# Reading out a linear-attention memory as one block of tiled matmuls instead of riders between gate/up matmuls

## The reference

```python
log_f_cum = jnp.cumsum(jax.nn.log_sigmoid(fg), axis=-1)
log_D = jnp.where(ltr, log_f_cum[..., :, None] - log_f_cum[..., None, :] + ig[..., None, :], -jnp.inf)
max_log_D = jnp.max(log_D, axis=-1, keepdims=True)
C = jnp.einsum('bhsd,bhtd->bhst', qh, kh) / jnp.sqrt(jnp.float32(dh)) * jnp.exp(log_D - max_log_D)
normalizer = jnp.maximum(jnp.abs(jnp.sum(C, axis=-1, keepdims=True)), jnp.exp(-max_log_D))
h = jnp.einsum('bhst,bhtd->bhsd', C / (normalizer + EPS_BACKEND), vh)
...
x = x + _L0_xattn_ref(_layernorm(x, axis=-1), ctx_1024, ctx_1024, ...)
x = x + _L0_ffn_ref(_layernorm(x, axis=-1), w_gate, w_up, w_down)   # fp4_linear: 512 -> 1408 (twice), silu(gate) * up, 1408 -> 512
```

## Time and profile before

| | |
|---|---|
| median of 3 runs | 1887.38 us (1887.36 to 1887.93) |
| the profiled execution | 1892.68 us, its span 1891.0 us |
| TensorE busy | 1783.6 us (94%), mean granted clock 0.971 |
| VectorE busy | 1566.1 us (83%) |
| ScalarE busy | 1415.8 us (75%) |
| GpSimd busy | 1191.7 us (63%) |
| one plain turn | 26.41 us |
| one gate turn | 28.98 us |

### The profile page before, as it was taken

The page is one execution under the profiler, slowest core; times in us unless marked ns, Lnnn a source line. Parts: engine busy times, 40 slices in busy tenths (PEclk is TensorE's granted clock), DMA queues, the critical chain, the costliest instruction groups (busy, mean ns, idle before and its releaser), DMA issues. The chain is left out here.

```text
span 1891.0 us, 36967 instructions
## 1 busy us (share of the span) xinstructions
PE 1783.6 (94%) x11513; PEld 1046.0 (55%) x11513; DVE 1566.1 (83%) x3213; ACT 1415.8 (75%) x2943; POOL 1191.7 (63%) x1189
## 2 busy tenths in 40 slices
PE   4557999999999999999999999999999999999996
PEld 3434556556555565555556555655565555555553
DVE  8987888888887888879888888888888888889993
ACT  7765777787877777777777877777787877776753
POOL 7765666566666656666666666656666665656652
PEclk8668999999999999999999999999999999999998
DMA  6334454344444534444444454444443454445332
GB/s 214 101 75 94 120 115 111 108 120 124 108 114 114 127 99 116 120 111 116 113 121 109 121 115 116 109 110 119 123 110 108 122 126 101 115 104 110 88 66 62
DMA packets 342116, 211.47 MB, mean 112 GB/s; under 512 B 275200, under 2 KB 281856, under 8 KB 341920
## 3 DMA queue, kind: packets, MB, share of 16 engines
q1 hardware_dynamic: 341920, 209.10, 44.1%
HBM read 125.93 MB, written 17.30 MB: 76 GB/s over the span
## 5 line engine op out<-in xcount | busy, mean ns | idle before, releaser
L485 PE MATMUL bank<-wgTh,xqT 128*128 128x512 f16 (+1 forms) x1536 | 556.9, 363 | 15.0 <-DMA xqT<-xqs 15.0
L485 PE MATMUL bank<-wuTh,xqT 128*128 128x512 f16 (+1 forms) x1536 | 556.6, 362 | 0.0
L1077 POOL TENSOR_TENSOR stage<-stage,hs 128x512 f32<-128x512 f32 (+1 forms) x192 | 190.4, 992 | 433.9 <-DVE stage L1286 433.9
L613 PE MATMUL bank<-wdTh,work 128*128 128x512 f16 x704 | 269.0, 382 | 12.3 <-DMA work<-stage 12.2
L485 PE MATMUL bank<-wgTl,xqT 128*128 128x512 f16 (+1 forms) x768 | 278.4, 362 | 0.0
L485 PE MATMUL bank<-wuTl,xqT 128*128 128x512 f16 (+1 forms) x768 | 278.1, 362 | 0.0
L614 PE MATMUL bank<-wdTl,work 128*128 128x512 f16 x704 | 267.7, 380 | 0.0
L615 PE MATMUL bank<-wdTh,work 128*128 128x512 f16 x704 | 267.4, 380 | 0.0
L485 PEld LDWEIGHTS bank<-wgTh,xqT 128*128 128x128 f16 x1536 | 157.1, 102 | 160.0 <-DMA xqT<-xqs 22.7
L1130 POOL TENSOR_TENSOR stage<-stage,hinv 128x512 f32<-128x512 f32 (+1 forms) x192 | 238.9, 1246 | 8.2 <-DVE hinv L1371 8.1
L485 PEld LDWEIGHTS bank<-wuTh,xqT 128*128 128x128 f16 x1536 | 163.8, 107 | 131.8 <-issue 1.1
(11 more groups left out here) (209 smaller groups left out, 3954.4 us busy)
## 6 DMA issues: line engine op xcount, KB each, us to landing
mb<-max_dram SPq DMA_DIRECT2D x64, 512.0 KB, 4.0
x<-in_x_dram SPq DMA_DIRECT2D x64, 256.0 KB, 2.9
cf<-in_ctx_dram SPq DMA_DIRECT2D x64, 256.0 KB, 3.7
cn<-in_ctx_dram SPq DMA_DIRECT2D x64, 256.0 KB, 3.8
wb<-warp_dram SPq DMA_DIRECT2D x128, 128.0 KB, 3.4
out_dram<-ob SPq DMA_DIRECT2D x64, 256.0 KB, 3.7
xb<-in_x_dram SPq DMA_DIRECT2D x60, 256.0 KB, 2.6
work<-stage SPq DMA_TRANSPOSE x192, 3.1
```

The lines of the kernel that those rows point to most:

```text
L485: i = e.matmul(o[:, 0:width], x, w[:, c, n0:n0 + width], start=first and k < 2, stop=last and k >= 4)
L613: e.matmul(DOWN[:, :], hi, wdT[0][:, c0 + c, :], start=(c0 + c == 0), stop=False)
L1077: e.tensor_tensor(blocks(hx[:, n0:n0 + w]), blocks(hx[:, n0:n0 + w]), per_block(hs2[:, n0 // BLOCK:(n0 + w) // BLOCK]), ALU.mult).then_inc ...
```

## The change

The riders go. u becomes a block of its own behind the third gate/up piece, followed at once by `pe_st_mm`, which was behind down part 0. Inside the block every product is cut to a half of the output rows (64 columns of the array). The product with the old memory reads `St` itself: 64 rows of one head by 64 columns, so that four such matmuls use the four quarters of the array (16 matmuls). The product of `D` and `vc` uses all 128 rows and one half of the columns each (16 matmuls). `U` is laid out anew: even heads in bank R2, odd heads in bank R0, and `act_uc` writes with a stride. `Sbd`, its two copies per tile and its semaphores go. The memory is updated in one pass of four instructions, one for each head pair (`St*wb + ST`), at the place of the old `dve_St`; `sp_wb_in` waits for it.

```diff
-        U = [b[:, 0:HC * DA].rearrange("p (c r d) -> p c r d", r=2, d=DA) for b in (R2, R0)]
+        U = [b[:, 0:HC * DA].rearrange("p (c d) -> p c d", d=DA) for b in (R2, R0)]
+        HALF = [slice(0, P // 2), slice(P // 2, P)]
...
             if t.has(1):
-                e.wait_ge(S_["Sd"], t.done(1))
+                e.wait_ge(S_["St"], t.done(1))
                 e.wait_ge(S_["xw"], t.done(1))
...
-                    if n == 2 and c >= 2 and t.has(2) and rider.live(NT):
-                        pe_u_part(e, rider, 6 * (c - 2) + k)
...
-        def pe_u_part(e, t, k):
...
-            c, j = divmod(k, 3)
-            o = U[c // 2][:, c % 2]
-            if j == 0:
-                return e.matmul(o.rearrange("p r d -> p (r d)"), xw[:, c, :], Sbd[:, c, :, :].rearrange("p r d -> p (r d)"),
-                                start=(c % 2 == 0), stop=False)
-            i = e.matmul(o[:, j - 1, :], D[:, j - 1, c, :], vc[t.parity][:, 2 * c + j - 1, :], start=False, stop=(c % 2 == 1 and j == 2))
...
+        def pe_u(e, t):
...
+            if t.has(8):
+                e.wait_ge(S_["St"], t.done(8))
+            e.wait_ge(S_["xw"], t.done())
+            for c in range(HC):
+                for half in HALF:
+                    for par in range(2):
+                        r = slice(par * DH, (par + 1) * DH)
+                        e.matmul(U[par][half, c, :], xw[r, c, half], St[t.slot][r, c, :], start=(c == 0), stop=False)
+            e.wait_ge(S_["vc"], t.done())
+            e.wait_ge(s_C[0], t.done())
+            e.wait_ge(s_C[1], t.done())
+            for c in range(HC):
+                for par in range(2):
+                    for half in HALF:
+                        i = e.matmul(U[par][half, c, :], D[:, par, c, half], vc[t.parity][:, 2 * c + par, :], start=False, stop=(c == HC - 1))
+            i.then_inc(S_["u"], 1)
...
             if t8.live(NT):
                 pe_gu(e, t8, 2)
+            if t6.live(NT):
+                pe_u(e, t6)
+                pe_st_mm(e, t6)
             if t9.live(NT):
                 pe_down(e, t9, 0)
-            if t6.live(NT):
-                pe_st_mm(e, t6)
...
-        def act_Sbd(e, t, par):
...
-            e.copy(uc[:, HC * k:HC * (k + 1), :], U[k].rearrange("p c r d -> p (c r) d")).then_inc(s_uc[k], 1)
+            e.copy(uc[:, :, :].rearrange("p (c r) d -> p r c d", r=2)[:, k], U[k]).then_inc(s_uc[k], 1)
...
-        def dve_Sd(e, t):
+        def dve_St(e, t):
...
             e.wait_ge(S_["wb_in"], t.of(32, 31))
+            e.wait_ge(S_["u"], t.done())
+            e.wait_ge(S_["st_mm"], t.done())
...
-            e.tensor_tensor(St[t.slot][:, :, :], St[t.slot][:, :, :], per_head(wb[:, :, P - 1], DA), ALU.mult).then_inc(S_["Sd"], 1)
...
-            e.tensor_tensor(St[t.slot][:, :, :], ST, St[t.slot][:, :, :], ALU.add).then_inc(S_["St"], 1)
+            for c in range(HC):
+                i = e.scalar_tensor_tensor(St[t.slot][:, c, :], St[t.slot][:, c, :], wb[:, c, P - 1:P], ST[:, c, :], ALU.mult, ALU.add)
+            i.then_inc(S_["St"], 1)
```

More of the change, by code:

```diff
@@ L259, in mlstm_fp4_ffn @@
             "row3", "row4", "mc", "row_T", "cols",
-            "D", "xw", "vc", "vk", "qk", "u", "st_mm", "Sd", "St", "sq", "un",
+            "D", "xw", "vc", "vk", "qk", "u", "st_mm", "St", "sq", "un",
             "nrm", "vr", "ve", "sch", "hn", "x1",
@@ L275, in mlstm_fp4_ffn @@
         s_gu, s_silu, s_h = ([S_[f"{k}{n}"] for n in range(NP)] for k in ("gu", "silu", "h"))
-        s_mask, s_C, s_uc, s_Sbd = ([sem(f"s_{k}{n}") for n in range(2)] for k in ("mask", "C", "uc", "Sbd"))
+        s_mask, s_C, s_uc = ([sem(f"s_{k}{n}") for n in range(2)] for k in ("mask", "C", "uc"))
         s_hx, s_hz, s_h_t, s_h_q, s_h_qs, s_h_hi = ([sem(f"s_{k}{n}") for n in range(NP)] for k in ("hx", "hz", "h_t", "h_q", "h_qs", "h_hi"))
@@ L474, in pe_gu @@
                 e.wait_ge(s_h[n + 1], t.done(1))
-            rider = t.back(-2)
             for c in range(EC):
@@ L557, in pe_pick_mm @@
                 i.then_inc(S_["pick_mm"], 1)
-        def pe_u_part(e, t, k):
+        def pe_u(e, t):
             later = t.back(-5)
[L562 to L574, removed]
-            c, j = divmod(k, 3)
-            o = U[c // 2][:, c % 2]
-            if j == 0:
-                return e.matmul(o.rearrange("p r d -> p (r d)"), xw[:, c, :], Sbd[:, c, :, :].rearrange("p r d -> p (r d)"),
-                                start=(c % 2 == 0), stop=False)
-            i = e.matmul(o[:, j - 1, :], D[:, j - 1, c, :], vc[t.parity][:, 2 * c + j - 1, :], start=False, stop=(c % 2 == 1 and j == 2))
-            return i.then_inc(S_["u"], 1) if k == 11 else i
@@ L583, in pe_u @@
-        def pe_u(e, t):
-            for k in range(12):
-                pe_u_part(e, t, k)
+            if later.live(NT + 1) and later.slot % 4 == 0 and later.has(4):
+                e.wait_ge(S_["cols"], later.quads(4))
+            if later.live(NT):
+                e.wait_ge(S_["xT"], later.done())
+                if later.at_start(7):
+                    e.wait_ge(S_["gr"], later.quads_of(4, 3))
+            if t.at_start(0):
+                e.wait_ge(S_["zero"], 1)
+            if t.has(8):
+                e.wait_ge(S_["St"], t.done(8))
@@ L1048, in act_start @@
             e.preload_act_table_set(EXP_LN); act_f_exp(e, T[7]); act_uc(e, T[2], 1); act_x_hi(e, T[1]); act_f_log(e, T[7]); act_uc(e, T[2], 0); act_hz(e, T[0], 1)
-            act_sq(e, T[2]); act_D(e, T[3]); act_warp(e, T[7]); act_hz(e, T[0], 2); act_hz(e, T[0], 0); act_ln1_sq(e, T[8]); act_Sbd(e, T[3], 1)
-            act_silu(e, T[1], 0); act_h_hi(e, T[0], 0); act_nm2(e, T[2]); act_Sbd(e, T[3], 0); act_sq2(e, T[2]); act_ln1_var(e, T[8]); act_var2(e, T[2])
+            act_sq(e, T[2]); act_D(e, T[3]); act_warp(e, T[7]); act_hz(e, T[0], 2); act_hz(e, T[0], 0); act_ln1_sq(e, T[8])
+            act_silu(e, T[1], 0); act_h_hi(e, T[0], 0); act_nm2(e, T[2]); act_sq2(e, T[2]); act_ln1_var(e, T[8]); act_var2(e, T[2])
             act_x1c(e, T[2]); act_silu(e, T[1], 1); act_xh(e, T[8]); act_h_hi(e, T[0], 1); act_silu(e, T[1], 2); e.preload_act_table_set(EXP_LN)
@@ L1176, in pool_zero @@
                 e.memset(St[i][:, :, :], 0.0)
-            e.memset(Sbd[:, :, :, :], 0.0)
             for i in range(2):
@@ L1615, in dve_turn @@
                 dve_x_t(e, t7)
-            if t6.live(NT):
-                dve_Sd(e, t6)
             if t1.live(NT):
@@ L1699, in dve_start @@
             dve_x_q(e, T[2]); dve_ht(e, T[1]); dve_nr_neg(e, T[3]); dve_h_lo(e, T[0], 2); dve_nr(e, T[3]); dve_nq(e, T[3]); dve_vr(e, T[3]); dve_hm(e, T[1])
-            dve_n2(e, T[3]); dve_x_lo(e, T[2]); dve_ve(e, T[3]); dve_Sd(e, T[3]); dve_hinv(e, T[1]); dve_St(e, T[3]); dve_hn(e, T[3])
+            dve_n2(e, T[3]); dve_x_lo(e, T[2]); dve_ve(e, T[3]); dve_hinv(e, T[1]); dve_St(e, T[3]); dve_hn(e, T[3])
         @block.vector
```

31 lines of the change are left out of this document (10 added, 21 removed).

## The result

The changed kernel has a median of 1878.33 us (1876.42 to 1880.88, 6 runs) against 1889.52 us for the kernel before on the same chips; the ratio is 0.9939, 95% interval 0.9923 to 0.9956. It is faster by 0.6%, where 1.8% was forecast, and 1878.33 us lies 1.3 us above the range. The profiled execution went from 1892.7 to 1876.4 us: 16.3 us, where the sum said 33.3.

The account below looks back on a forecast made before the run. TensorE's list was taken to bound each turn; plain turns 29.1, late transposes 4.1, tail turns 3.6, gate turns -3.5 and start-up 0 sum to 33.3 us gained: 1859.4 us profiled, 1854 median (-1.8%), range 1842 to 1877.

Parts of the forecast that it names:

- each term of the block: New TensorE block: memory product 0.47, D times vc 0.94, pe_st_mm 0.47, changes of form 0.36; together 2.24 us against 2.95.
- four quarters at once: Memory product in the new block: 32 records, four at a time, 8 steps, taken as 0.47 us; bounds up to 1.87.
- The third `act_silu`: ScalarE in plain turns: silu 2 moves up 1.2 us and no more, because it waits 1.19 us for TensorE.
- The rival of pairs: Memory product's quarters run two at a time: 0.94 us, gain 0.24 us a turn, 1876 us; chance 0.14 including an in-between case.
- the serial quarters: Rival: quarters in the memory product don't overlap, 1.87 us, block 3.64 us; slower, 1925 us; chance 0.11.
- The rule of some 25 ns between starts: Skill's limit on matmul starts: the memory product's 32 records would need 0.80 us, gain 0.38 us a turn.
- The sentence on SyncE's wait for the update: SyncE's wait for St before wb_in stands behind the x transpose, issue 1.2 us, so St is done by then.
- The bound of -2 to +2 us: Start-up put at 0 within these bounds: VectorE and ScalarE lose short instructions, but the first update stands later.
- Late transposes: Plain turns: the x transpose's margin grows from 1.04 to 1.5 us, covering the 1.4 us excess; 4.1 us gained.
- VectorE's 1.28 us: Plain turns: VectorE loses the 1.28 us decay pass, 1.2 as a step, so its work moves up 1.2 us.
- Gate turns: In 14 turns the scores wait for St, which ends 0.76 us after its start; each 0.25 us longer, -3.5 us.
- The base: Profiled execution of 1892.7 us, 5.3 above the median; the same gain was taken from both, giving 1859.4 and 1854 us.

Follow-up runs that it names:

- e1: Changed kernel with the load of tile 3's decay factors moved behind tile 1's x transpose in SyncE's start-up list; 1865.19 us, ratio 0.9863 to the kernel before.

## Why the prediction was wrong

- **The bound was read right in plain turns.** TensorE's list sets a plain turn in both kernels, and each term of the block held: 2.27 us against 2.24, turns of 25.74 against 25.70. The one term without a row, four quarters at once, went as taken: groups of four 0.058 us apart behind a first step of 0.11. The third `act_silu` moved up 1.25 us, 1.2 forecast. The rival of pairs (0.24 us of gain a turn) and the serial quarters (slower, 1925 us) fell with it. The rule of some 25 ns between starts (the Trainium skill, "TensorE: Matmul & The Clock Gate", "Wait — 56ns, not 53.3ns?") would have given 0.80 us for these records; they come one per 15 ns on average (32 starts within 0.48 us), so as a mean rate it doesn't hold for matmuls in different quarters.
- **The steps that failed.** The sum missed by 17.0 us: 5.9 in the late transposes, 5.8 in the start-up, 3.4 in the gate turns and 1.9 in the plain turns, of which there was also one fewer to count.
- **The start-up** (0 forecast, -5.8 us). The sentence on SyncE's wait for the update was worked out for a turn of the loop, where it is true (e1 doesn't change turns). It wasn't worked out for the start-up list, where the same line stands in another order: there the update comes 13 us too late and eight weight transposes are queued behind the wait. The bound of -2 to +2 us had no row behind it. Without the stall the start-up would have given +8 to +10 us (e1), which was not in the sum either.
- **Late transposes:** the sum took 4.1 us of lateness as won, on the ground that the margin grows from 1.04 to 1.5 us while a slow transpose takes 1.4 more. Both halves were off. In plain turns the margin stayed at 1.07 us (median; 0.6 to 1.4) where it had been 1.04, and the long transposes of x take 1.6 to 1.9 us more; four of the 14 long ones of the kernel before already took over 4.8 us. And it took their number as given. The change adds TensorE instructions, and with them instruction packets; with 6.98 of them to a cycle of four turns a bad place stayed bad from 1000 us to the end of the loop. The late gate turns (5.9 us in all before, 6.6 after) had no term.
- **VectorE's 1.28 us:** the decay pass was so long because GpSimd's product `vk` ran beside it. Between 300 and 1700 us it takes 1.28 us in the 38 turns in which the two overlap and 0.42 in the 13 in which they don't. With the pass gone, `dve_h_lo` stands there and takes 1.33 us in 39 turns with that overlap and 0.67 in 13 without, so `dve_x_lo` begins 20.92 us into a plain turn instead of 21.62 (medians), 0.70 us earlier and not 1.2. The turn is 0.67 us shorter, and so the margin stayed.
- **Gate turns:** mechanism right, size off. The prediction had the scores waiting for St and a turn 0.25 us longer; it is 0.44. Four instructions of 65 elements step by 0.19 us instead of 0.17, so the update lasts 0.85 us instead of 0.76, and the scores start 0.15 us behind its end where 0.05 was put, although the kernel before shows 1037.30 - 1037.16 = 0.14.
- **The base:** the profiled execution of before was 5.3 us above the median of its first three runs, 3.2 above that of all six (1889.52); that of after was at the lowest of its runs, 1.9 below. Carrying a gain from one profiled execution to the median hides such a difference: the profiles are 16.3 us apart, the medians 11.2.

## What to carry to other kernels

When a wait is moved to a later event, look up every place where the waiting instruction stands, the start-up list too, and everything behind it in its queue: this one line cost 13 us of the changed kernel (e1) and nothing in the loop. When the bound engine gets faster, the next wait is often one that already had a fraction of a microsecond of margin; here the cure was to let an idle engine drain the PSUM region, so that the bound engine doesn't wait for the consumer of its data. Float32 matmuls with few moving columns (65 here) are paced by their weight load; cut them into column halves and row halves that write different partitions and banks, and stand them together.

## What was new about the hardware

- Four quarters of the array (64 rows by 64 columns, float32, 65 moving columns) run at once: 32 records start within 0.48 us. Behind a first step of 0.11 us a group of four costs 0.058 us, as much as a pair of column halves; a single record of 128 by 128 costs 0.112.
- A DMA transpose of 3.05 us takes 4.3 to 5.1 us in some of the cases in which a packet of TensorE's instructions is loaded while it runs (25 of 256 transposes in the changed kernel, 26 before, all with such a packet), and the number of instructions per loop cycle decides whether that happens at the same place in every cycle (6.98 packets) or in every fourth (5.75).
- A VectorE pass over two SBUF operands of 260 elements takes 0.42 us alone and 1.28 us while GpSimd's product runs.
